# The down product's first group: VectorE order written out, two h buffers for six units, rows of x1 ahead of an h load

## The reference, cut to what matters

```python
x = L0_attn_x                              # (4, 512, 1024) f32
x = x + _L0_attn_ref(_layernorm(x))        # attention over the 4 rows of the batch: x1
Wg, Wu, Wd = (NF4_CODE[q] * absmax per block of 64)   # Wg, Wu (3584, 1024), Wd (1024, 3584)
g = x_norm @ Wg.T ; u = x_norm @ Wu.T
h = silu(g) * u                            # (4, 512, 3584)
return x + h @ Wd.T                        # x here is x1
```

## Time and profile before

| What | Value |
|---|---|
| Median of 3 runs | 1755.41 us (1754.37 to 1755.49) |
| The profiled execution's own time | 1756.18 us |
| Its span, first to last instruction | 1754.4 us |
| PE busy with matmuls | 1641.2 us (94%) |
| DVE, ACT busy | 1221.6 us (70%), 1031.3 us (59%) |
| TensorE's granted clock, mean | 0.975 |
| Down product on PE | from 1213.88 us to 1749 us |
| First group, units 0 to 7 | 1213.88 to 1305.63 us |
| Last group, units 32 to 39 | from 1633.5 us |

### The profile page before, as it was taken

The page is one execution under the profiler, slowest core; times in us unless marked ns, Lnnn a source line. Parts: engine busy times, 40 slices in busy tenths (PEclk is TensorE's granted clock), DMA queues, the critical chain, the costliest instruction groups (busy, mean ns, idle before and its releaser), DMA issues.

```text
span 1754.4 us, 20118 instructions
## 1 busy us (share of the span) xinstructions
PE 1641.2 (94%) x7840; PEld 789.6 (45%) x7840; DVE 1221.6 (70%) x1564; ACT 1031.3 (59%) x1116; POOL 68.9 (4%) x98
## 2 busy tenths in 40 slices
PE   5874589999999999999999999999699999999898
PEld 5762334444444444444444444444244444444343
DVE  7788556668576685766856767577677757577566
ACT  5644476767676676767767677688586625343000
POOL 3143100000000000000000000000000000000000
PEclk9996899999999999999999999999899999999999
DMA  6231023223242241422414233144654435343573
GB/s 256 84 126 66 0 90 102 102 91 126 79 156 91 90 141 64 156 91 100 146 49 156 91 114 132 51 153 154 232 188 167 166 140 194 126 167 131 203 266 123
DMA packets 76911, 226.39 MB, mean 129 GB/s; under 512 B 5264, under 2 KB 19984, under 8 KB 76304
## 3 DMA queue, kind: packets, MB, share of 16 engines
q1 hardware_dynamic: 76816, 225.10, 35.8%
HBM read 156.93 MB, written 68.16 MB: 128 GB/s over the span
## 4 chain that ended last, share of the span: by engine, by line
PE 84%; DVE 8%; ACT 3%; DMA 3%; issue 1%; SPq 0%; POOL 0%; DVEq 0%; ACTq 0%; POOLq 0%
PE ps L1446 19%; PE ps L1447 19%; PE ps L1448 19%; PE ps L1564 9%; PE ps L1566 9%; PE ps L1565 9%; ACT codes L624 1%; PE ps L1415 1%; DMA codes<-q_dram 1%; DVE stats L900 1%; DVE tmp L972 1%; DMA xb<-x_dram 1%; DVE xa L1094 1%; DMA gs<-h_dram 0%; DMA h_dram<-rw 0%
## 5 line engine op out<-in xcount | busy, mean ns | idle before, releaser
L624 ACT ACTIVATE codes<-codes 128x1024 f32<-128x1024 f32 (+1 forms) x672 | 708.2, 1054 | 158.6 <-DMA codes<-q_dram 144.6
L1446 PE MATMUL ps<-xa,wg 128*128 128x512 f16 x392 | 150.4, 384 | 24.5 <-DVE xa L1094 19.4
L1292 DVE SCALAR_TENSOR_TENSOR xb<-ps,y_back,xb 128x512 f32<-128x512 f32 x140 | 103.8, 749 | 82.6 <-PE ps L1566 78.4
L1446 PE MATMUL ps<-xb,wg 128*128 128x512 f16 x392 | 149.6, 382 | 11.4 <-DVE rw L1110 11.4
L1446 PE MATMUL ps<-xb,rw 128*128 128x512 f16 x392 | 148.6, 379 | 4.2 <-ACT gs L694 2.6
L1447 PE MATMUL ps<-xa,wg 128*128 128x512 f16 x392 | 150.3, 384 | 0.0
L1448 PE MATMUL ps<-xa,wg 128*128 128x512 f16 x392 | 150.3, 383 | 0.0
L1447 PE MATMUL ps<-xb,wg 128*128 128x512 f16 x392 | 149.6, 382 | 0.0
L1448 PE MATMUL ps<-xb,wg 128*128 128x512 f16 x392 | 149.4, 381 | 0.0
L1446 PE MATMUL ps<-xa,rw 128*128 128x512 f16 x392 | 149.1, 380 | 0.0
L1447 PE MATMUL ps<-xa,rw 128*128 128x512 f16 x392 | 149.1, 380 | 0.0
(11 more groups left out here) (265 smaller groups left out, 3021.6 us busy)
## 6 DMA issues: line engine op xcount, KB each, us to landing
codes<-q_dram SPq DMA_DIRECT2D x84, 512.0 KB, 4.7
absm<-a_dram SPq DMA_DIRECT2D x69, 512.0 KB, 3.8
h_dram<-rw SPq DMA_DIRECT2D x28, 1024.0 KB, 4.2
gs<-h_dram SPq DMA_DIRECT2D x21, 1344.0 KB, 5.9
h_dram<-rw SPq DMA_DIRECT2D x28, 768.0 KB, 4.9
rw<-h_dram SPq DMA_DIRECT2D x11, 896.0 KB, 6.1
rw<-x_dram SPq DMA_DIRECT2D x16, 512.0 KB, 11.1
xa<-a_dram SPq DMA_DIRECT2D x13, 512.0 KB, 6.2
```

Source lines behind the costliest of these rows:

```text
L624: fn(real, real if step else whole, ACT.Prelu, bias=at0, scale=slope, alpha=left).then_inc(bends_done, 1)
L1292: return v.scalar_tensor_tensor(out=dst, in0=ps[:, bank, :], scalar=y_back[:, 0:1], in1=dst, op0=ALU.mult, op1=ALU.add)
L1446: mm(dst, w_hi, x_hi, start=(start and kt == 0), stop=False, skip_group_check=True)
```

## The change

It touches only the down product.

- `UNIT_OF_JOB`: job 61 moves from unit 2 to unit 3.
- `STEPS`: ACT makes 6 bends in unit 2 and 3 in unit 3 (before: 3 and 6). The sum over units 0 to 7 and the order of the bends stay.
- `h_slot`: units 0 to 5 use the h buffers 0 and 1, units from 6 on the other three. `load_h` of units 2 to 5 waits for the unit two before; those of 6 to 8 for `hlo2_done` of slot 55.
- SP's order: in unit 1 `load_h(3)` stands ahead of `load_after(60)`; `store_h(54)` is in unit 2 and `store_h(55)` in unit 4, each ahead of that unit's `load_after`; each of units 0 to 5 loads h of the unit two ahead, unit 6 those of units 8 and 9. In unit 32 the rows 1 to 3 of x1 are issued ahead of `load_h(35)`, before behind it.
- `store_out`: the half with columns 2 and 3 is stored first, when 3 of the unit's 4 final operations are done; the other when all 4 are. Before, both waited for 4.
- ACT: `h_high(54)` and `h_high(55)` stand behind first1 of units 1 and 3 (before: at the end of units 1 and 2), and the 3 bends of units 1 and 3 behind first3. Unit 2 waits for w_done of one more job.
- DVE: the first group is written out. `add_c22(2)` stands ahead of `h_sums(55)` and of job 61 (only `weight_halves(60)` and `h_low(54)` are still between it and `add_c22(1)`); job 61 is begun ahead of `add_c22(3)` and ended behind it, then comes `h_low(55)`; `add_c22` of units 4 and 5 stands ahead of their jobs, as those of units 6 and 7 did before.

```diff
@@ -21,7 +21,7 @@
 UP_JOBS = 4 * NP
 
 DOWN_JOBS = UP_JOBS + 4
-UNIT_OF_JOB = {1: 60, 2: 61, 4: 62, 5: 63, 6: 64, 7: 65, 9: 66, 10: 67, 11: 68, 12: 69, 13: 70, 14: 71,
+UNIT_OF_JOB = {1: 60, 3: 61, 4: 62, 5: 63, 6: 64, 7: 65, 9: 66, 10: 67, 11: 68, 12: 69, 13: 70, 14: 71,
                17: 72, 18: 73, 19: 74, 20: 75, 21: 76, 22: 77, 25: 78, 26: 79, 27: 80, 28: 81, 29: 82, 30: 83}
 
 ACT_HIGH = 4
@@ -33,7 +33,7 @@
 UNITS = 8
 NV = NG * UNITS
 
-STEPS = (6, 3, 3, 6, 6, 6, 6, 4)
+STEPS = (6, 3, 6, 3, 6, 6, 6, 4)
 
 DOWN_BANKS = ((5, 6, 7, 0), (2, 3, 1, 4))
 
@@ -319,10 +319,10 @@
 
         def h_slot(v):
 
-            if v < 4:
+            if v < 6:
                 return v % 2, 16 * (v // 2 + 1)
-            t = (v - 4) % 3
-            return 2 + t, (32 if t == 2 else 16) * ((v - 4) // 3 + 1)
+            t = (v - 6) % 3
+            return 2 + t, (32 if t == 2 else 16) * ((v - 6) // 3 + 1)
 
         def pair_blocks(t, n, part):
 
@@ -429,9 +429,9 @@
                     sp.wait_ge(p5_done, SLOTS - 1)
                 elif v == 1:
                     sp.wait_ge(p4_done, SLOTS - 1)
-                elif v < 4:
+                elif v < 6:
                     sp.wait_ge(d3_done, v - 1)
-                elif v < 7:
+                elif v < 9:
                     sp.wait_ge(c12_done, SLOTS)
                     sp.wait_ge(c22_done, SLOTS)
                     sp.wait_ge(hlo2_done, 2 * NP)
@@ -467,8 +467,8 @@
                                  .rearrange("p (e t) -> p e t", e=2)).then_inc(row_in[u % 4], 16)
 
             def store_out(u):
-                sp.wait_ge(final, 4 * u + 4)
-                for half in range(2):
+                for half in (1, 0):
+                    sp.wait_ge(final, 4 * u + 4 - half)
                     sp.dma_start(out_v[ORDER[2 * (u // B) + half], u % B].rearrange("p (e t) -> p e t", e=2),
                                  x1_buf[u % 4][:, 2 * half:2 * half + 2, :]).then_inc(out_done, 16)
 
@@ -483,24 +483,25 @@
             for c in range(CT):
                 sp.wait_ge(x1_out[c], 16)
             for v in range(NV):
+                if v == 1:
+                    load_h(v + 2)
+                elif v in (2, 4):
+                    store_h(SLOTS - 3 + v // 2)
                 if v in UNIT_OF_JOB:
                     load_after(UNIT_OF_JOB[v])
-                if v < 2:
+                if v in (0, 2, 3, 4, 5):
                     load_h(v + 2)
-                elif v == 2:
-                    store_h(SLOTS - 2)
-                    store_h(SLOTS - 1)
-                    load_h(4)
-                    load_h(5)
-                elif v == 3:
-                    load_h(6)
-                elif v + 3 < NV:
+                elif v == 6:
+                    load_h(8)
+                    load_h(9)
+                elif v == NV - UNITS:
+                    for u in range(1, 4):
+                        load_row(u)
+                    load_h(v + 3)
+                elif 6 < v < NV - 3:
                     load_h(v + 3)
                 if v == NV - UNITS - 2:
                     load_row(0)
-                elif v == NV - UNITS:
-                    for u in range(1, 4):
-                        load_row(u)
                 if v >= NV - UNITS:
                     u = v - NV + UNITS
                     store_out(u)
@@ -857,29 +858,32 @@
                     act.wait_ge(p2_done, SLOTS - 1)
                     act.wait_ge(p3_done, SLOTS - 1)
                 elif t == 2:
-                    act.wait_ge(w_done, UP_JOBS + 3)
+                    act.wait_ge(w_done, UP_JOBS + 4)
                 elif t == 3:
                     act.wait_ge(p3_done, SLOTS)
                 act.wait_ge(d1_done, t + 1)
                 take(b1, 3, t).then_inc(first1_done, 1)
-                for k, step in now[:2]:
-                    bend(k, step)
+                if t in (1, 3):
+                    h_high(SLOTS - 2 + t // 2)
+                else:
+                    for k, step in now[:2]:
+                        bend(k, step)
                 act.wait_ge(d2_done, t + 1)
                 take(b1, 0, t).then_inc(first2_done, 1)
-                for k, step in now[2:4]:
-                    bend(k, step)
+                if t not in (1, 3):
+                    for k, step in now[2:4]:
+                        bend(k, step)
                 act.wait_ge(d4_done, t + 1)
                 act.wait_ge(add5_done, t + 1)
                 take(b5, 2, t).then_inc(first4_done, 1)
-                for k, step in now[4:5]:
-                    bend(k, step)
+                if t not in (1, 3):
+                    for k, step in now[4:5]:
+                        bend(k, step)
                 act.wait_ge(d3_done, t + 1)
                 act.wait_ge(add7_done, t + 1)
                 take(b7, 1, t).then_inc(first3_done, 1)
-                for k, step in now[5:]:
+                for k, step in now if t in (1, 3) else now[5:]:
                     bend(k, step)
-                if t in (1, 2):
-                    h_high(SLOTS - 3 + t)
             for k, step in left[at:]:
                 bend(k, step)
 
@@ -1320,30 +1324,44 @@
                 dve.wait_ge(*sum_done(t - UNITS, first3_done, add3_done))
                 add(b7, 1, t).then_inc(add3_done, 1)
 
-            def unit(t):
+            def weights_begin(k):
+                scale_codes(k)
+                sum_blocks(k)
+
+
+            add_c22(0)
+            h_sums(SLOTS - 2)
+            weights_begin(DOWN_JOBS)
+            add_c22(1)
+            weight_halves(DOWN_JOBS)
+            h_low(SLOTS - 2)
+            add_c22(2)
+            h_sums(SLOTS - 1)
+            weights_begin(DOWN_JOBS + 1)
+            add_c22(3)
+            weight_halves(DOWN_JOBS + 1)
+            h_low(SLOTS - 1)
+            add_c22(4)
+            weights_begin(DOWN_JOBS + 2)
+            weight_halves(DOWN_JOBS + 2)
+            add_c22(5)
+            weights_begin(DOWN_JOBS + 3)
+            weight_halves(DOWN_JOBS + 3)
+            add_c22(6)
+            weights_begin(DOWN_JOBS + 4)
+            weight_halves(DOWN_JOBS + 4)
+            add_c22(7)
+            weights_begin(DOWN_JOBS + 5)
+            weight_halves(DOWN_JOBS + 5)
+
+            for t in range(UNITS, NV - UNITS):
                 k = UNIT_OF_JOB.get(t)
-                late = t in (UNITS - 2, UNITS - 1)
-                if k is not None and not late:
-                    scale_codes(k)
-                    sum_blocks(k)
+                if k is not None:
+                    weights_begin(k)
                 add_c22(t)
-                if late:
-                    scale_codes(k)
-                    sum_blocks(k)
                 if k is not None:
                     weight_halves(k)
-                if t >= UNITS:
-                    add_rest(t)
-
-            unit(0)
-            h_sums(SLOTS - 2)
-            unit(1)
-            h_low(SLOTS - 2)
-            h_sums(SLOTS - 1)
-            unit(2)
-            h_low(SLOTS - 1)
-            for t in range(3, NV - UNITS):
-                unit(t)
+                add_rest(t)
 
             def last_bank(bank, src, row, e):
 
```

## The result

The changed kernel takes 1734.65 us (median of 4 runs, 1733.41 to 1735.74), the kernel before, beside it, 1754.89: ratio 0.9884, interval 0.9869 to 0.9898, 20.2 us less. The forecast was 1733.0 in a range of 1729 to 1739.5. The profiled execution took 1733.68, its span is 1731.9. Two executions that took far longer than all others (6153.28 us of e2, 2531.26 us of the kernel before beside e5 to e8) are left out of every median here.

What follows compares the result with a forecast made beforehand. PE was busy 94% of the span, so only its waits or slow clock were worth time. Savings of 14.4 + 6.8 + 1.2 = 22.4 us took the profiled 1756.18 to 1733.8, median 1733.0; range 1729 to 1739.5.

Steps and rivals of the forecast that it cites:

- Part 1: First group of the down product: DVE's order and h buffers remove both long waits; 14.4 us less after new losses.
- Codes of job 62 come late and hold first1 of unit 2: Unit 2: codes issued near 1233.0 behind the h load delay ACT's bend and take, so PE waits ahead of d2.
- Size of that wait: PE ahead of d2 of unit 2: 4.0 us, with codes landing at 1239.5; bounds 1.9 and 8.7.
- Rival A: Unit 2: the new wait is absent or short (1.9 us, no clock change); 1730, or 1728 without any; chance 0.14.
- Clock behind it: Slow PE clock after the new wait in unit 2: 0.8 us taken, bounds 0 and 1.86.
- First group: Waits and slow clock in the down product's first group: 19.2 us lost before, 4.0 + 0.8 after, 14.4 less.
- Nothing later late: Units after unit 2: no further waits counted; first1 of unit 4 has half a microsecond of margin.
- Part 2: Unit 33: x1 rows issued ahead of the h load remove idle and slow clock; 6.8 us less, bounds 0 and 6.8.
- Part 3: Last unit: storing one half earlier leaves one store at the end; 1.2 us less, bounds 0.4 and 1.3.
- B: First group: a second wait, for first1 in unit 4 or h of unit 6, costing 5 us; 1738; chance 0.17.
- C: Unit 33: the x1 row is late anyway, so only the first group's gain comes; 1740; chance 0.04.
- D: Units 4, 5, 6 and 8: each h load becomes a wait ahead of d1, 7.5 us each; 1763; chance 0.03.

Runs made afterwards that it cites:

- e2: Kernel before with only rows 1 to 3 of x1 issued ahead of load_h(35): 1748.04 us, ratio 0.9964.
- e5: Changed kernel, SP still waiting for unit 1's end but then issuing absmax and codes of job 62 ahead of load_h(3): 1729.45 us, ratio 0.9856.
- e8: Changed kernel with VectorE's order in the first group as before: 1740.33 us, ratio 0.9919.
- e7: Changed kernel with the h buffers as before (units 0 to 3 in two buffers, later units in the other three): 1746.34 us, ratio 0.9951.
- e1: Changed kernel with absmax and codes of job 62 issued ahead of load_h(3) in unit 1, as before the change: 1726.24 us, ratio 0.9841.
- e6: Changed kernel where SP waits until the codes of job 62 have landed before storing slot 54: 1733.94 us, one execution.
- e9: Kernel of e1 with one bend of job 65 moved from unit 7 to unit 6: 1726.16 us, ratio 0.9833.
- e3: Kernel before with only the two halves of each output row stored apart, columns 2 and 3 first: 1752.26 us, one execution.
- e4: Changed kernel with both edits of the last group undone (x1 rows and halves of a store): 1742.71 us, ratio 0.9935.
- e10: Changed kernel with the bend that waits for the codes of job 62 moved behind first1 of unit 2: 1733.26 us, one execution.

## Why the prediction was right

- **Part 1, both long waits go**: right. Unit 3 waits for nothing at its end, and unit 4's h is there. e7 and e8 show that both the h buffers and VectorE's order are needed for the whole gain; ScalarE's moves (`h_high`, `STEPS`) were not run alone.
- **Codes of job 62 come late and hold first1 of unit 2**: right in place, cause, chain (ACT's bend, its take, PE's d2) and time of issue (1233.0 forecast; 1230.83, or 1233.1 when the down product's earlier start, 2.3 us, is added back). e1 takes it away by SP's order alone.
- **Size of that wait**: forecast 4.0 us, measured 4.7 by PE's row (4.9 start to start: 1239.75 against unit 2's start 1229.70 + 5.18). The landing is the term that was mis-sized: 6.5 us taken, 7.2 measured; the stores behind account for 0.5 (e6). The forecast had put the cost of the store at nothing. The rule cited there, of the Trainium skill, DMA: Bandwidth & Descriptors (Queues, rings and completion order), is about order; that a transfer behind another is free for it was my step, and e6 does not bear it out. The row that the forecast used for it hints at a price: those codes of 1243.55, with both stores right behind, landed in 5.6 us, against a median of 4.8.
- **The other 0.2 of the landing** fits the forecast's allowance for issues closer together, which the runs don't bear out. h, absmax and codes of job 62 took 7.7 us from first issue to last landing before, 7.5 in e1 and 7.9 in e9 (codes issued 1.55 us behind h), 7.6 in e6 (0.93 behind), and 8.2 in the changed kernel, where the forecast had 6.9 to 7.7. (Rival A says of this trio that it took 6.14; that is the landing of the codes alone.)
- **Clock behind it**: this term was mis-sized. Forecast 0.8 with bounds 0 and 1.86; measured 16.21 - 9.07 - 4.88 = 2.3 us, outside its bounds. The granted clock fell to 0.5 and 11 matmuls ran at 0.43 us. The row of unit 4, 1.86, was no upper bound: it is 9 slow matmuls. Unit 2 of the kernel before had 11, as the changed kernel has, and lost 18.41 - 9.07 - (1245.59 - 1238.49) = 2.2 us by them; its rows are in the earlier trace rows.
- **First group**: forecast 14.4 less, measured 12.1; the 2.3 missing are the wait (0.9 too small) and the clock behind it (1.5 too small).
- **Nothing later late**: right. first1 of unit 4 was done at 1259.42, and PE's d2 was due at 1254.97 + 5.18 = 1260.15: 0.7 us to spare, where 0.5 had been worked out. h of units 6 and 8 came in time.
- **Part 2**: 6.8 forecast and measured; e2 has it alone (6.3 by the medians, wait gone in the trace).
- **Part 3**: forecast 1.2, measured 1.3 in the trace of the changed kernel and in e3. (The forecast's own two ends, 1754.05 and 1752.75, are 1.3 apart.)
- **Span**: 1732.0 forecast, 1731.9 measured, and this is partly luck: 2.3 us too much in the first group met 2.3 us by which the phases ahead of the down product happened to be shorter. The same luck is in "unit 7 ending near 1291.2" (measured 1291.23). The medians say 20.2 where 22.4 was forecast, and 1734.65 us where 1733.0 was.
- Of the rivals, A (short wait), B (a second wait) and C (the row late all the same) did not occur. D, slower by loads of h that all come late, did not either; e7 shows what one such wait costs, 8.74 us of idle.

What is not settled: why the start of the down product moves by up to 3 us between executions, and what decides whether the clock falls after an idle of some 3 us.

## What to carry to other kernels

Where DMAs are issued in program order, look for a call whose wait ends late and that stands ahead of one which is free to go and which PE will soon need: here two swapped calls cost 7.1 us of the 27 that the edit could give. When a reorder removes a long wait, follow each queue in program order to the next item that it now holds up; that gave the remaining wait to within a microsecond. And price a wait of PE of several microseconds with its slow matmuls: take the worst row of the trace for the bound, not the nearest.

## What the runs showed of the hardware

- After PE's idle of 4.16 to 4.74 us in unit 2 (changed kernel, e4, e6, e7, e8) PE ran at the lower of its two clock levels each time, for 10 to 12 matmuls (11 in the changed kernel, 1239.75 to 1244.40). After 1.57 (e5) it did not. After 3.34 (e10) eight were slow, and in e8 an idle of only 2.78 us was followed by six at 0.43 us (the window above: mean clock 0.55). An idle of 2.63 us in the gate phase of the kernel before (PE back at 255.31) had no slow matmul behind it.
- Two stores (1 MB and 0.75 MB), issued 1.6 and 3.3 us behind a 512 KB load on the same queue, made that load land 0.5 us later (7.2 against 6.7 in e6).
- The codes (512 KB) landed 4.6 us after their issue with absmax (512 KB) alone in front (e5, where h was issued 0.5 us behind them and the stores later), 6.7 with 0.9 MB of h in front too and nothing behind (e6), and 7.2 with h in front and the stores behind (changed kernel).
